# A transformer block's experts: all experts for all tokens, or sorted tokens in 128-slot tiles

## The reference

```python
x = x + attention(layernorm(x))
xc = layernorm(x).astype(bfloat16)
normed = rms_norm(xc) * norm_weight                        # bfloat16
logits = normed @ gate_weight.T + gate_bias
scores, idx = top_k(logits, 2); w = softmax(scores)
combine = sum(one_hot(idx, 8) * w)                         # two of eight are not zero
p1 = einsum('bsh,eoh->bseo', normed, mlp1_weight) + mlp1_bias      # 256 -> 512, each expert
g, lin = min(p1[..., 0::2], 7), clip(p1[..., 1::2], -7, 7)
act = g * sigmoid(1.702 * g) * (lin + 1)
p2 = einsum('bsei,ehi->bseh', act, mlp2_weight) + mlp2_bias        # 256 -> 256, each expert
out = x + (xc + einsum('bseh,bse->bsh', p2, combine).astype(bfloat16))
```

## Time and profile before

| | us |
|---|---|
| median of 3 runs | 1219.71 (1218.33 to 1222.45) |
| profiled execution, its own time | 1218.1 |
| its span, first to last instruction | 1216.3 |
| head, to the first exponential | 88.5 |
| attention of units 0, 1, 2, 3 | 86.0, 142.4, 131.0, 153.4 |
| attention of units 4, 5, 6, 7 | 133.7, 153.2, 103.3, 103.4 |
| behind the last exponential | 121.4 |

### The profile page before, as it was taken

One profiled execution on the slowest core, in us unless ns is written; L12 is line 12 of the kernel. 1 busy time (PEld: TensorE's weight loads), 2 busy tenths in 40 slices (PEclk: granted clock), 3 DMA queues, 4 the chain that ended last, 5 costly groups with the idle time before them and its releaser, 6 DMA issues.

```text
span 1216.3 us, 17776 instructions
## 1 busy us (share of the span) xinstructions
PE 974.2 (80%) x5241; PEld 414.5 (34%) x5313; DVE 861.2 (71%) x1702; ACT 699.3 (57%) x905; POOL 400.5 (33%) x344
## 2 busy tenths in 40 slices
PE   4719897879678997898578898887878999996575
PEld 2402222234232443333233343323333444344243
DVE  5723204768658896786586899586966997898797
ACT  2318895746458574764447675664657776771232
POOL 2413304422244334433135334441321333233243
PEclk9759998989899999988799998998989999997686
DMA  4253342303424241333403334241323442411010
GB/s 148 81 111 59 90 90 63 91 27 79 102 53 105 65 100 58 84 82 76 105 26 84 79 91 101 53 109 44 91 67 77 99 105 58 99 41 39 31 52 31
DMA packets 56443, 92.72 MB, mean 76 GB/s; under 512 B 7162, under 2 KB 41346, under 8 KB 53250
## 3 DMA queue, kind: packets, MB, share of 16 engines
q1 hardware_dynamic: 37892, 66.14, 24.0%
q10 hardware_dynamic: 18432, 25.17, 7.1%
HBM read 74.24 MB, written 17.04 MB: 75 GB/s over the span
## 4 chain that ended last, share of the span: by engine, by line
PE 47%; DVE 28%; issue 12%; ACT 4%; DMA 3%; POOL 2%; SPq 2%; another core or an unknown queue 1%; DVEq 0%; ACTq 0%; POOLq 0%
PE OP L644 12%; PE S L630 11%; PE D L616 7%; DVE th_sb L1052 3%; PE A L599 3%; PE D L543 3%; PE BB L599 3%; DVE act_sb L1057 3%; DVE g_sb L1035 3%; PE D L526 2%; DVE acc L1047 2%; DVE l_sb L1037 2%; ACT probs L761 2%; DMA X<-in_x 2%; DVE xn L895 2%
## 5 line engine op out<-in xcount | busy, mean ns | idle before, releaser
L761 ACT ACTIVATE probs<-S 128x1024 f32<-128x1024 f32 x512 | 511.9, 1022 | 245.9 <-PE S L630 239.5
L630 PE MATMUL S<-Qs,Ks 98*128 98x512 bf16 x1024 | 311.9, 397 | 66.1 <-issue 28.5
L644 PE MATMUL OP<-probs,V 128*17 128x512 f32 x2048 | 280.6, 621 | 2.7 <-ACT O L770 2.7
L848 POOL TENSOR_TENSOR act_lo<-act_sb,act_hi 128x512 fp32r<-128x512 f32 x128 | 165.0, 1289 | 224.9 <-DVE act_hi L1063 164.6
L616 PE MATMUL D<-W,act_hi 128*128 128x256 f32 x448 | 138.3, 338 | 40.9 <-DVE Vn L935 20.0
L630 PEld LDWEIGHTS S<-Qs,Ks 98*128 98x128 bf16 x1024 | 80.2, 100 | 252.9 <-issue 95.6
L1047 DVE SCALAR_TENSOR_TENSOR acc<-D,combh,acc 128x256 f32<-128x256 f32 x224 | 97.3, 476 | 79.7 <-PE D L616 79.6
L616 PE MATMUL D<-W,act_lo 128*128 128x256 f32 x448 | 119.0, 295 | 0.0
L842 POOL TENSOR_SCALAR W<-W2b 128x512 fp32r<-128x512 bf16 x64 | 44.2, 690 | 225.7 <-PE D L616 220.8
L737 ACT ACTIVATE th_sb<-g_sb 128x512 f32<-128x512 f32 x128 | 80.1, 626 | 64.0 <-DVE g_sb L1035 63.2
L1052 DVE SCALAR_TENSOR_TENSOR th_sb<-th_sb,g_sb 128x512 f32<-128x512 f32 x128 | 116.3, 909 | 0.1
(11 more groups left out here) (138 smaller groups left out, 1063.4 us busy)
## 6 DMA issues: line engine op xcount, KB each, us to landing
W<-in_w ACTq DMA_DIRECT2D x64, 256.0 KB, 2.7
Ks<-k_scr SPq DMA_DIRECT2D x32, 384.0 KB
W2b<-in_w ACTq DMA_DIRECT2D x64, 128.0 KB, 2.7
Ks<-k_scr SPq DMA_DIRECT2D x32, 256.0 KB
q_scr<-parts SPq DMA_DIRECT2D x16, 384.0 KB, 2.8
k_scr<-parts SPq DMA_DIRECT2D x16, 384.0 KB, 2.5
Qs<-q_scr SPq DMA_DIRECT2D x32, 192.0 KB
X<-in_x SPq DMA_DIRECT2D x8, 512.0 KB, 7.6
```

The costliest lines, as they stand in the source:

```text
L630: last = mm(S[:, j2, C * i:C * (i + 1)], Ks[0:SROWS + MROWS, g % 2, j, P * kt:P * (kt + 1)], Qs[0:SROWS + MROWS, g % 2, j, :], start=True, ...
L644: last = mm(OP[32 * j:32 * j + VW, :], V[:, kt, HG * g + j, :], probs[:, s % 2, C * j:C * (j + 1)], start=kt == 0, stop=kt == KT - 1)
L761: nc.scalar.activation(probs[:, s % 2, 2 * C * j2:2 * C * (j2 + 1)], S[:, j2, :], ACT.Exp, scale=SCALE).then_inc(exp_done, 1)
L848: tt(act_lo[:, e % 2, it, :], act_sb[:, a % 2, :], act_hi[:, e % 2, it, :].bitcast(FP32), ALU.subtract).then_inc(lo_s, 1)
```

## The change

Each token's row goes only to its two experts. Tokens of a unit are sorted by expert into slots: expert e gets ceil(count / 128) tiles of 128 slots. 1024 choices fill at most NT = 15 tiles, and all 15 are always computed, in NPAIR = 8 pairs (the last has one tile).

- Gates: `sel` and a stage `rank` (half 30): eight small matmuls on PE count, for each token and expert, the tokens before it; `place_slots` on DVE makes slot numbers `pos` and the tiles' experts `eid` in 15 small operations.
- `scatter` (half 33, POOL): 8 indirect DMAs of 128 rows of 512 bytes from `nf` to DRAM `xs`.
- `wl` (SP): for each tile of a pair loads the expert's number from `eid` to a register, then W1 (256 KB) and W2 (256 KB, now float32 that was converted once at the start and lies in DRAM `w2f`). Four tile buffers. It waits for the `down` of pair m - 2.
- `xg` (SP): loads a pair's slots; `gx` (PE transposes them into D, DVE copies out); `up`: per tile 4 blocks of 128 channels, each a bias matmul (9 rows) and two matmuls of 128 columns; g and l moved out for both tiles in 512 columns; tanh, hidden, lo as before, once a pair; `down`: 4 matmuls 128x256 per tile; DVE copies to `ysb`; `store` (SP) writes it to DRAM `ys`.
- `gather` (POOL): 8 indirect DMAs of 128 rows of 1 KB from `ys` to `yg`; `combine` (DVE): 8 multiply-adds into acc, with the weights `wsel`.
- Places: pair m has its base at half 40 + 6m: wl at -4, xg at -3, gx at 0, up at +2, tanh +3, hidden +4, lo +5, down +8, store +9. b2 at 86 and 88, gather at 92, combine 96, final 97, so FINAL = 48.

```diff
-NF = 2 * NE
+NT = C * TOPK // P + NE - 1
+NPAIR = (NT + 1) // 2
...
-    FFN0, LAG, PAIRED = 26, 4, True
-    DOWN, TANH, HIDDEN, UP, LO, W2AT = 0, 2, 2, 1, 5, 3
+    FFN0, PACE = 40, 6
+    WL, XG, TANH, HIDDEN, LO, DOWN, STORE = -4, -3, 3, 4, 5, 8, 9
+    UP = 2
...
+                elif st == "wl":
+                    wait_apart(sp, (gating, GATING * u + TILED))
+                    if not looped(u) and u == 0 and a == 0:
+                        wait_apart(sp, (w2_w, 32))
+                    if looped(u) or u or a >= 2:
+                        wait_apart(sp, (m2_mm, NPAIR * u + a - 1))
+                    for q in range(tiles_of(a)):
+                        t, to = 2 * a + q, 2 * (a % 2) + q
+                        e = sp.value_load(eid[0:1, t:t + 1], min_val=0, max_val=NE - 1)
+                        sp.dma_start(W1[:, to, :, :], w1[bass.ds(e, 1)].rearrange("o p c n -> (o p) c n")).then_inc(w_ld[a % 2], 16)
+                        sp.dma_start(W2[:, to, :].bitcast(FP32), w2f[bass.ds(e, 1)].rearrange("o p n -> (o p) n")).then_inc(w_ld[a % 2], 16)
+                elif st == "xg":
+                    sp.wait_ge(sc_s, 16 * TOPK * TC * (u + 1))
+                    if looped(u) or u or a >= 2:
+                        sp.wait_ge(xgT_s, NPAIR * u + a - 1)
+                    nt = tiles_of(a)
+                    sp.dma_start(xg[:, a % 2, 0:nt, :], xs[n][2 * P * a:2 * P * a + P * nt, :].rearrange("(q p) c -> p q c", p=P)
+                                 ).then_inc(xg_ld[a % 2], 16)
...
+                elif st == "gx":
+                    pe.wait_ge(xg_ld[a % 2], rows_in(u, a))
+                    for q in range(tiles_of(a)):
+                        for c in range(CT):
+                            i = CT * q + c
+                            last = nc.tensor.transpose(bank[:, :].bitcast(BF16)[:, P * i:P * (i + 1)], xg[:, a % 2, q, P * c:P * (c + 1)],
+                                                       identb[:, :])
...
+                for q in range(tiles_of(m)):
+                    for k in range(BLOCKS):
+                        cols = slice(P * k, P * (k + 1))
+                        mm(bank[:, q, cols], b1_sb[:, cols], oneh[:, 2 * m + q:2 * m + q + 1].to_broadcast([NE + 1, P]), start=True, stop=False)
+                        for c in range(CT):
+                            r = P * (CT * q + c)
+                            last = mm(bank[:, q, cols], W1[:, 2 * (m % 2) + q, c, cols], xgT[:, m % 2, r:r + P],
+                                      start=False, stop=c == CT - 1)
...
+                elif st == "scatter":
+                    wait_apart(pool, (gating, GATING * u + PLACED), (nf_s, TC * (u + 1)))
+                    if not looped(u) and u < NCH:
+                        wait_apart(pool, (xs_z, 16 * NCH))
+                    for k in range(TOPK):
+                        for t in range(TC):
+                            i = TC * k + t
+                            nc.gpsimd.indirect_dma_start(xs[n], bass.IndirectOffsetOnAxis(ap=pos[:, n, i:i + 1], axis=0),
+                                                         nf[:, t, :], None).then_inc(sc_s, 16)
+                elif st == "gather":
+                    wait_apart(pool, *((y_w[i], rows_in(u, NPAIR - 1)) for i in range(2)))
+                    for t in range(TC):
+                        for k in range(TOPK):
+                            i = TC * k + t
+                            nc.gpsimd.indirect_dma_start(yg[:, t, k, :], None, ys[n],
+                                                         bass.IndirectOffsetOnAxis(ap=pos[:, n, i:i + 1], axis=0)).then_inc(yg_ld[t], 16)
```

More of the change, by code:

```diff
@@ L80, in block_kernel @@
         place(POST, AT[f"wo{a}"], ("wo", a))
[L81 to L100, removed]
+    for m in range(NPAIR):
+        h = FFN0 + PACE * m
+        for st, off in (("wl", WL), ("xg", XG), ("gx", 0), ("up", UP), ("tanh", TANH), ("hidden", HIDDEN), ("lo", LO),
+                        ("down", DOWN), ("store", STORE)):
+            place(EXPERTS, h + off, (st, m))
+    h = FFN0 + PACE * (NPAIR - 1) + DOWN
+    for a in range(2):
+        place(EXPERTS, h - 4 + 2 * a, ("b2", a))
+    place(EXPERTS, h + 2, ("gather", 0))
+    place(EXPERTS, h + 6, ("combine", 0))
+    place(EXPERTS, h + 7, ("final", 0))
+    FINAL = (h + 7) // 2
+    ORDER = ("gx", "up", "down", "tanh", "hidden", "lo", "store", "wl", "xg", "b2", "gather", "combine", "final")
     for l in EXPERTS.values():
@@ L559, in stage @@
                     last.then_inc(d_full, 1)
+                elif st == "rank":
+                    pe.wait_ge(gating, GATING * u + GATES1)
+                    each, width = sel[:, :, :].rearrange("p t e -> p (t e)"), TC * NE
+                    mm(bank[:, 0:width], tri[:, :], each, start=True, stop=False)
+                    for d in range(1, TC):
+                        mm(bank[:, NE * d:width], ones[:, :], each[:, 0:width - NE * d], start=False, stop=d == TC - 1)
+                    for t in range(TC):
+                        last = mm(bank[:, width:width + NE], ones[:, :], each[:, NE * t:NE * (t + 1)], start=t == 0, stop=t == TC - 1)
+                    last.then_inc(d_full, 1)
                 elif st == "combT":
-                    pe.wait_ge(comb_s, 3 * (u + 1))
+                    pe.wait_ge(comb_s, u + 1)
                     for t in range(TC):
@@ L614, in expert_down @@
+                _, bank = pair_banks(u, m)
+                for q in range(tiles_of(m)):
                     for k in range(4):
                         it, part = k // 2, (act_hi, act_lo)[k % 2]
[L616 removed]
+                        r = FI * q + P * it
+                        last = mm(bank[:, E * q:E * (q + 1)], part[:, m % 2, r:r + P], W2[:, 2 * (m % 2) + q, E * it:E * (it + 1)],
@@ new lines, in place_slots @@
+                for i in range(3):
+                    link(v.tensor_tensor(ends[i + 1][:, NE:2 * NE], ends[i][:, NE:2 * NE], ends[i][:, NE - 2 ** i:2 * NE - 2 ** i], ALU.add))
+                end = ends[3]
+                link(v.scalar_tensor_tensor(slot[:, :, :], end[:, None, NE - 1:2 * NE - 1].to_broadcast([P, TC, NE]), float(P), before,
+                                            ALU.mult, ALU.add))
+                link(v.tensor_tensor(slot2[:, :, :, :], slot[:, None, :, :].to_broadcast([P, TOPK, TC, NE]), chosen[:, :, :, :], ALU.mult))
@@ new lines, in combine @@
+            def combine(u, n):
+                dve.wait_ge(acc_s, 2 * (u + 1))
+                for k in range(TOPK):
+                    for t in range(TC):
+                        if k == 0:
+                            dve.wait_ge(yg_ld[t], 16 * TOPK * (u + 1))
+                        else:
+                            dve.wait_ge(comb2_s, TOPK * TC * u + t + 1)
+                        v.scalar_tensor_tensor(acc[:, t, :], yg[:, t, k, :], wsel[:, n, k, t:t + 1], acc[:, t, :],
+                                               ALU.mult, ALU.add).then_inc(comb2_s, 1)
```

336 lines of the change are left out of this document (199 added, 137 removed), and 2 rows, old and new, of the table AT.

## The result

The changed kernel takes **1616.9 us** (median of 4 runs, 1609.5 to 1620.9) against 1219.7: ratio 1.325, 95% interval 1.318 to 1.331. It is slower, as forecast, but by 397 us, not by 65, and outside the range. The profiled run took 1620.7 us, its span is 1618.8.

The account below looks back on a forecast made before the run. PE, full beside experts with DVE nearly so, was taken as the bound. Middle +22 (-79 work, +234 stalls, -133 absorbed), tail +39 and start +4 made +65: 1218.1 to 1283 us, range 1125 to 1370.

Parts of the forecast that it names:

- This decides: SP's new chain, 6.3 us against 3.7 of PE work: PE stops 2.6 us at 45 pairs, +117 us.
- the 39 for the loads of a group ahead: SP, pairs 2 and 5 of a unit: wl behind a group's loads costs 3 us more, 13 times, +39.
- The faster rival, 0.36: SP chain is covered, deciding from a chain of 4 us down: -70, 1148 us, or some 1125; chance 0.36.
- I take 0.056, so 1.34 us: PE, first layer of a pair: 24 matmuls of 128 columns at 0.056 us each, 1.34 us.
- the -79: PE's work beside attention: 1.52 us less for each of 52 pairs, -79 us.
- Middle: -79 + 234 - 133: Units with attention and experts: PE's saved work, plus stalls, minus idle time absorbing them, +22 us.
- I let it all be absorbed: -133: PE's present idle time beside attention, 133 us, takes up that much of the 234 us of stalls.
- 12 us late in six units: Gathers and scatters on POOL delay a unit's first slots 12 us in six units, 6 in the first: +78.
- The POOL rival: POOL's indirect DMAs collide with other work, 2.5 us each instead of 1.3: about +100, 1383 us; chance 0.10.
- the stall is the same one: Rope work on POOL queues behind the batches, PE's products behind that; counted as the same stall, no extra cost.
- Unit 6's late pairs take about the time of its late f's: Tail's front: unit 6's remaining pairs last about as long as the old kernel's expert pieces (f's) there.
- a pair's loop is some 10 us: Tail: transposes, copy, both layers, SP 3.6 and landing 2.7 make some 10 us per pair, six loops.

Follow-up runs that it names:

- the gathers in between: Changed kernel with slots asked for first, bias over 128 rows, and gathers, combination and last additions 3 half steps later: 1381.6 us, ratio 1.132 to before.
- the two edits: Changed kernel with slots asked for ahead of store and weights, and bias matmul over 128 rows, gathers unmoved: 1371.2 us, ratio 1.126 to before.

## Why the prediction was wrong

**The direction and the mechanism held.** "This decides", said of the chain through SP: it is the largest wait, and taking the order away gives back 120 us against the 117 priced for it. That nearness is partly luck. The wait in the pure steps was 3.3 to 3.7 where 2.6 was forecast, with 8.8 and 5.1 in place of 6.3 and 3.7. Only 28 of the 45 pairs had such a wait (PE waits for the slots 133 us in the middle, of which 25 at two first pairs), so the 117 and the 39 for the loads of a group ahead were 108 in all. And a part of the 120 is clock.

**The faster rival, 0.36, did not come.** It asked for a chain of 4 us. The chain was 8.8: weights 3.3 after the second layer's end, the store 0.5, landing 4.9. The forecast's 6.3 had the weights' part right (3.5). It left out the store of pair m - 2, which stands between wl and xg in the queue, and took the landing from the weights' row of the kernel before, 2.7. With nothing just ahead of them the slots land in 2.1; behind four weight loads and a store they take 4.3 in the median. The price went by a row of the kernel before, not by what the change itself puts ahead of this load.

**"I take 0.056, so 1.34 us" is the first step that failed.** It is a term of the sum that was mis-sized. The first layer took 2.88. The row it came from holds eight matmuls that all have 128 rows, and at 128 rows the 0.056 was right (0.055). What the row couldn't show is that each third matmul of the burst has 9 rows, and that the switch costs 0.17 to 0.20. So "1.52 less per pair" was nothing (4.04 against 4.06 us, with 2.88, 0.96 and 0.22): PE's work did not fall at all, the -79 was +1. (The check of the unit prices against the stretch has a slip as well: it sets 0.88 for a step's scores where the row has 0.96. With that the sum is 9.9 and not 9.6, against 9.5.) The 81 ns that TensorE: Matmul & The Clock Gate of the Trainium skill gives for such a matmul, weighed there, agrees with neither: 55 in a burst of one row count, 120 in the mixed one.

**"Middle: -79 + 234 - 133" is the second.** All of this sum was at full clock. The stalls were priced at their own length, and the same stretch of the profile says that a kernel whose PE pauses some 3.5 us at more than half of its pairs has a granted clock of 0.82. That is up to 138 us that no term held. The kernel before had the hint: in its tail, where PE is busy 59% of the time, the clock was 0.73.

**"I let it all be absorbed: -133" is the third.** Full absorption would have left PE idle for the stalls alone, 234. It is idle for 279.2. Of these 133 are for the slots; the other 146 have other releasers, 58 of them the exponentials. The 133 us of before were thus replaced rather than used up, and how much of a slot wait fell into them can't be told apart here.

**Scatter and gather.** 1.3 us apiece against 1.25 measured: right. "12 us late in six units": PE waits for the first pair's slots in units 6 and 7 alone, 11.4 and 13.3 us (steps of 15.2 and 17.5 us). The POOL rival is false: 0.30 us between indirect transfers and no gap of 6 us beside them. But "the stall is the same one" was a slip. In units 2 to 5 PE loses the time ahead of the first pair, in two steps of some 14 and 8.8 us (unit 1, without gathers, has 8.9 and 9.2), and both go through ACT's queue, where a copy of the rotation's results stands ahead of the exponentials. Unit 4:

```profile
808.03 0.62 ACT L793 CAST parts<-rot 128x512 bf16<-128x512 f32 x1 [11.78 <-POOL rot L893]
...
819.62 0.62 ACT L799 CAST parts<-sw 128x512 bf16<-128x512 f32 x1 [6.31 <-POOL sw L896]
```

The first does not come from the gathers in POOL's queue, as the prediction and the theory of the gathers in between have it. On DVE a shuffle for the rotation stands behind the computing of the slots and the combination of the gathered rows (until 803.4), POOL's rotation waits 7.5 us for it, and PE pauses 6.9 us before 810.20. The second is the subtraction behind the eight scatters. The run with the gathers later made the second longer (18.7 us) than the first became shorter (8.7).

**The tail, +112 in place of +39**, comes apart into three. Forecast and found: first pair 67.6 us after the last exponential, and 101.5. Seven more pairs 63 and 98. The end 30 and 34.

```profile
1392.45 0.59 PE L652 MATMUL D<-identb,xg 128*128 128x128 bf16 x4 [5.31 <-DMA xg<-xs]
1407.46 0.59 PE L652 MATMUL D<-identb,xg 128*128 128x128 bf16 x4 [7.70 <-DMA xg<-xs]
1422.98 0.59 PE L652 MATMUL D<-identb,xg 128*128 128x128 bf16 x4 [8.22 <-DMA xg<-xs]
1424.09 3.42 PE L610 MATMUL D<-wo_sb,Op 128*128 128x256 f32 x8 [0.52 <-DVE xgT L1069]
...
1487.09 0.58 PE L652 MATMUL D<-identb,xg 128*128 128x128 bf16 x4 [18.11 <-DMA xg<-xs]
...
1510.23 0.59 PE L652 MATMUL D<-identb,xg 128*128 128x128 bf16 x4 [8.22 <-DMA xg<-xs]
```

"Unit 6's late pairs take about the time of its late f's" was the slip at the front: three of them stand ahead of the projection (L610) in PE's queue, each with a whole SP chain, 15.0 and 15.5 us apart; the projection starts 38.5 us behind the last exponential, 14 later than before. Then unit 6's eight gathers stand ahead of unit 7's scatters on POOL (10 us, forecast for the middle and forgotten here). And "a pair's loop is some 10 us" was 15.4: weights 3.3, store 0.5, landing 4.4, transposes and copy 1.1, first layer 4.15 (24 matmuls at 0.173, half clock), second 1.9. With the two edits the tail is 185.

**The signs to look for.** DVE's fall, the largest wait and the price of the indirect transfers came as written, the ten at the first pair of a unit in two units. "PE busy falls by some 80 us" was the one that named the error: it rose by 166. A loop of 10 to 11 us per pair and a tail near 160 were wrong with it.

## What to carry to other kernels

Take a matmul's price from a row with the same number of rows *in the same order*: a small bias matmul put into a chain of full ones costs far more than its size says, and padding it with zeros to the full row count brought a third matmul down to the price of the others here. When a change puts a wait into PE's queue, price what PE does afterwards at half clock too. In a queue that only issues transfers, put the load that somebody waits for ahead of the waits of stores and prefetches, and price its landing behind the transfers that will be in flight ahead of it, not from a row of another queue; and before you move a batch of indirect transfers, follow what stands behind it through the other engines' queues.

## What the runs showed of the hardware that was not expected

- Alternating 9-row and 128-row matmuls of 128 columns: 0.120 us apiece at full clock and 0.173 at half; the same matmuls all over 128 rows: 0.055 and 0.104.
- In the pair shown the granted clock is 0.50 for 3.4 us after a pause of 3.3 us, twice within the pair's period, while it is 1.00 in most of the pause itself. Matmuls without use in such pauses raised it from 0.82 to 0.87 in the middle.
- 128 KB of slots land 2.0 to 2.2 us after their issue when nothing was issued in the 3.5 us before, and in 4.3 us (median) right behind four weight loads and a store of 256 KB each. The same holds in both orders of the queue.
- Indirect transfers of 128 rows on POOL: 1.25 us from start to start in most, with 0.95 to 1.0 busy and 0.30 between.
